# Linear attention in front of a routed MLP: phi(K)^T x summed in fp16 parts and multiplied by Wv once per batch, gate logits as key columns, output bias moved into the expert part

## The chip, the cores and the metric

The kernel runs on one core of one Trainium2 chip. The metric is the device time of the whole program in microseconds (us). The kernel before takes 1902.31 us, the median of three runs (1900.44, 1902.31, 1904.35).

Names used below: PE is TensorE, ACT is ScalarE, DVE is VectorE, POOL is GpSimd, SP is SyncE, which here only issues DMAs.

## The reference, cut to what is computed

```
x: [16 batches, 1024 tokens, 256]            xn = layernorm(x)
Q = phi(xn Wq^T + bq)   K = phi(xn Wk^T + bk)   V = xn Wv^T + bv      phi(t) = elu(t) + 1, 16 heads of 16
KV = sum over tokens of K V^T (per head)      Ksum = sum over tokens of K
attn = (Q KV) / (Q . Ksum + 1e-6), then @ Wo^T + bo
scores = xn @ gate_w (8 experts); softmax over experts; each expert takes its top 256 tokens of a batch
h = gelu(xin @ w1[e]) @ w2[e], weighted by the gate, added back to its tokens; the sum is cast to bfloat16
out = x + attn + moe
```

The precision of fp32 products is reached with fp16 operands split in a high and a low part: three products (high-high, high-low, low-high) stand for one.

## The kernel before, in words

The program has two parts. The first (the attention part) does the layer norm, the attention and the gate, batch by batch; n counts 16 batches (NB), and j the 8 tiles (NT) of 128 tokens in a batch. The second (the expert part) runs 64 quarters: `body(b, ...)` for b from 0 to 15, q from 0 to 3 (five steps in the last). A quarter takes 512 gathered tokens through one expert's two matrices.

All order is written out by hand. Each engine has one in-order list of instructions, and semaphores (`wait_ge(event, at(event, n, k))`) tie the lists together. In the attention part an iteration n works on two batches: the projections of batch n, and the output side of batch m = n - 2 (LAG). The engines' lists for one iteration are:

- PE, `body` at L1385: per tile j `project` (L1262: keys and values in one bank, 6 products of 512 columns and a bias product of 256 columns), `gate` (L1276, four narrow products into bank pG), `sum_kv` of tile j-2 (L1291, fp32, two products of 129 columns, the last one a column of ones that sums phi(K)); `q_part` (L1304) at j = 2, 3, 6, 7; and for batch m `denominators` (j = 0), `turn_kv` (two transposes, j = 1), `fold_o` (j = 2), `reciprocals` (j = 4), and four `output` (after j = 5, 6, 7 and at the end of the iteration).
- ACT, L855: `high` (fp16 high part of x), `keys` (L804: relu of -k from PSUM, a copy of keys and values from PSUM to SBUF, exp), `queries`, `shift`, `sums_out`, `blocks_out`, `folded_out`, and in iterations 1 to 8 (`scan`) four `piece` (maxima of the expert weights).
- DVE, `body` at L1141: `stats_of` and `moments_of` (layer norm of batch n+1), `low`, `k_feature` of tile j-1 (L1035), `q_feature`, `gate_max`, `gate_probs`, `invert`, `split_rest`, `divide`, `add_x`, and from iteration 5 on one part of the top-k search of the first four batches behind every tile (`top_slot`).
- POOL, L754: `centre` (x minus mean, eight per batch), `norm` (L710: variance to 1/sqrt, it waits for `moments_of`), `add_bo` (L748, output bias onto x, four per batch) and `blocks_of` (L730, eight small instructions: value bias, head mask, denominators' operand).

`k_feature` reads keys and exp from SBUF. `project` of tile j needs the copy of tile j-2 out of its PSUM bank (kv_done). SP transposes the fp16 rows by DMA (`turn`), and the transposed buffer of half h comes free when the gates of the batch before are done (`gated`).

In the expert part PE alternates `product1` (6 products of 512 columns) and `product2` (12 of 256 columns). `weigh` on DVE (L1810, four instructions) empties the two PSUM banks of a quarter, and the next quarter's first `product2` waits for it (y_done). From b = 4 on, DVE does `finish(b, q)` (L1830) right ahead of `weigh`: a cast of the expert sum to bfloat16 and one addition onto the attention result. For b < 8 DVE also runs a part of the top-k search behind each `hidden_low` (one of them right ahead of `finish`). These lines set the order there:

```
                        top_slot(b, q, 6)
                        if fin and q < 4:
                            finish(b, q)
...
                        weigh(b, q)
```

## Time and profile before

| | before |
|---|---|
| runs | 1900.44, 1902.31, 1904.35 us |
| median | 1902.31 us |
| profiled execution: span from first to last instruction | 1898.3 us |
| median less span | 4.0 us |
| busy: PE / DVE / ACT / POOL | 98% / 69% / 67% / 54% of the span |
| attention part | to about 542 us of the span |
| expert part | from about 543 us to the end |

The profiled execution is one more execution of the same program, of which the profile gives the span alone, no time of its own; what lies around the span is taken as the 4.0 us between it and the median. "Busy" is the time in which an engine has an instruction in work. A matmul's record includes its latency, so neighbouring records overlap: how long a step of PE or DVE takes is read from one start to the next.

### The profile page before, as it was taken

The numbers are of one execution on the slowest core, as the hardware profiler recorded it, in microseconds if no ns is written. First come the engines' busy times: TensorE is split into PE (matmuls) and PEld (weight loads), VectorE is DVE, ScalarE is ACT, GpSimd is POOL, SyncE is SP. The second block draws the span as 40 slices with busy tenths as digits, with TensorE's granted clock in tenths as the row PEclk, the third lists the DMA queues.
The fourth block names the chain that finished last, engine by engine and source line by source line (L and its number), as shares of the span: only waits on it lengthen the run. The fifth ranks groups of instructions, "written<-read, shape, count | busy, mean of one in ns | idle before, by whom it ended". The sixth has DMA issues, their size and how long they took to land. (4 is left out here: it accounts for less than half of the span.)

```text
span 1898.3 us, 38991 instructions
## 1 busy us (share of the span) xinstructions
PE 1863.2 (98%) x13562; PEld 1269.6 (67%) x13562; DVE 1300.6 (69%) x2611; ACT 1272.2 (67%) x2045; POOL 1026.2 (54%) x947
## 2 busy tenths in 40 slices
PE   6899999999999999999999999999999999999998
PEld 4566666666676666666666666666666666666666
DVE  6678999998857777655787875555555555555556
ACT  6988887777746666666666666666666666666664
POOL 5656565656445555654455455545554554555453
PEclk9999999999999999999999999999999999999999
DMA  6979897989675555666677667576766766676857
GB/s 174 231 221 247 216 251 240 225 236 254 190 191 132 122 120 123 148 179 150 165 157 181 154 158 183 135 177 151 192 152 160 169 143 180 155 187 154 183 120 223
DMA packets 448900, 338.22 MB, mean 178 GB/s; under 512 B 224757, under 2 KB 430330, under 8 KB 448762
## 3 DMA queue, kind: packets, MB, share of 16 engines
q1 hardware_dynamic: 383674, 253.84, 48.5%
q0 software_dynamic: 48864, 66.88, 19.8%
q10 hardware_dynamic: 16224, 15.73, 2.5%
q8 instruction: 77, 1.26, 0.3%
q14 instruction: 61, 0.50, 0.1%
HBM read 185.61 MB, written 100.40 MB: 151 GB/s over the span
## 5 line engine op out<-in xcount | busy, mean ns | idle before, releaser
L1961 PE MATMUL pY<-w2s,hid 128*128 128x256 f16 x6144 | 756.6, 273 | 0.8 <-DVE hid L1806 0.8
L1946 PE MATMUL pH<-xgT,w1s 128*128 128x512 f16 (+1 forms) x3120 | 747.7, 376 | 1.3 <-PEq L324 1.3
L1961 PEld LDWEIGHTS pY<-w2s,hid 128*128 128x128 f16 x6144 | 599.8, 98 | 180.6 <-DVE yo L1822 3.6
L1806 DVE SCALAR_TENSOR_TENSOR hid<-gel,cur,hid 128x512 f16<-128x512 f32 (+1 forms) x520 | 384.6, 740 | 446.4 <-ACT hid L1745 440.8
L1720 POOL DMA_INDIRECT acc<-yo,idx x254 | 405.9, 1598 | 523.0 <-DVE yo L1822 450.0
L1742 ACT ACTIVATE gel<-pH,cur 128x512 f32<-128x512 f32 (+1 forms) x520 | 353.8, 680 | 476.7 <-PE pH L1946 457.2
L1946 PEld LDWEIGHTS pH<-xgT,w1s 128*128 128x128 f16 x3120 | 305.1, 98 | 252.4 <-DMA xgT<-xg 1.6
L1745 ACT ACTIVATE hid<-gel,cur 128x512 f16<-128x512 f32 (+1 forms) x520 | 372.0, 715 | 17.1
L219 POOL DMA_INDIRECT xg<-table,idx x256 | 286.1, 1118 | 112.1 <-issue 58.2
L1270 PE MATMUL pP<-wkv,xT 128*128 128x512 f16 x768 | 201.8, 381 | 7.8 <-DVE bias_rows L981 4.7
L724 POOL TENSOR_SCALAR xm<-xring,moments 128x256 f32<-128x256 f32 x128 | 120.9, 954 | 72.3 <-DVE xhl L1002 72.2
L1822 DVE TENSOR_SCALAR yo<-pY,gains,cur 128x256 f32<-128x256 f32 x256 | 121.6, 538 | 14.0 <-PE pY L1961 12.3
L1270 PEld LDWEIGHTS pP<-wkv,xT 128*128 128x128 f16 x768 | 75.0, 98 | 74.6 <-issue 9.5
L807 ACT ACTIVATE ek<-pP,winv_neg 128x256 f32<-128x256 f32 x128 | 61.2, 478 | 59.4 <-PE pP L1270 58.9
L1317 PE MATMUL pQ<-xT,wq 128*128 128x512 f16 x384 | 93.2, 378 | 2.1 <-ACT qraw L819 2.1
L208 DVE SCALAR_TENSOR_TENSOR w2s<-stage,cur,w2s 128x1024 f16<-128x1024 f32 x64 | 82.8, 1294 | 17.8 <-ACT w2s L200 17.8
L208 DVE SCALAR_TENSOR_TENSOR w1s<-stage,cur,w1s 128x1024 f16<-128x1024 f32 x64 | 82.8, 1294 | 17.9 <-ACT w1s L200 17.9
L752 POOL TENSOR_TENSOR x2ring<-x2ring,rows_all 128x512 f32<-128x512 f32 x64 | 87.1, 1390 | 3.8 <-DMA x2ring<-in_x 3.8
L809 ACT ACTIVATE kv<-pP,winv 128x512 f32<-128x512 f32 x128 | 88.6, 692 | 0.0
L1299 PEld LDWEIGHTS pKV<-kv,phik 128*128 128x128 f32 x512 | 74.4, 191 | 13.9 <-DVE phik L1039 0.7
L1032 DVE TENSOR_TENSOR qring<-qraw,eq 128x512 f32<-128x512 f32 x64 | 50.2, 785 | 46.6 <-ACT eq L821 46.3
L1299 PE MATMUL pKV<-kv,phik 128*128 128x129 f32 x512 | 75.6, 275 | 0.3 <-DVE phik L1039 0.3
(236 smaller groups left out, 1888.5 us busy)
## 6 DMA issues: line engine op xcount, KB each, us to landing
stage<-in_w SPq DMA_DIRECT2D x160, 512.0 KB, 6.4
xring<-in_x SPq DMA_DIRECT2D x16, 1024.0 KB, 6.4
x2ring<-in_x SPq DMA_DIRECT2D x16, 1024.0 KB, 7.6
table<-xhl SPq DMA_DIRECT2D x32, 512.0 KB, 4.1
mix<-x2ring SPq DMA_DIRECT2D x32, 512.0 KB, 3.0
acc<-zeros SPq DMA_DIRECT2D x16, 1024.0 KB, 4.6
fmix<-mix SPq DMA_DIRECT2D x48, 256.0 KB, 3.5
facc<-acc SPq DMA_DIRECT2D x48, 256.0 KB, 4.0
```

Source lines behind the costliest of these rows:

```text
L208: nc.vector.scalar_tensor_tensor(out=part_dst(i, 1, r), in0=staged(r), scalar=cur[i][:, 2 + r // 2:3 + r // 2], in1=part_dst(i, 0, r), op0 ...
L219: nc.gpsimd.indirect_dma_start(xg[i][:, s, :, :, :].rearrange("p a c t -> p (a c t)"), None, table, bass.IndirectOffsetOnAxis(ap=idx[q % 4 ...
L724: g.tensor_scalar(xm[:, j % HALF, :], xring[:, n % XR, j, :], moments[:, j, 0:1], None, ALU.subtract).then_inc(xm_done, 1)
L1270: last = t.matmul(pP[j % 2][:, :], xT[h][:, a, c, cols], wkv[:, b, c, :], start=k == 0 and c == 0, stop=k == 2 and c == DC - 1, skip_group ...
L1299: last = t.matmul(pKV[:, c * (P + 1):(c + 1) * (P + 1)], phik[:, j % 4, c * P:(c + 1) * P], kv1[:, j % 4, DC + c, :], start=j == 0 and c = ...
L1720: g.indirect_dma_start(acc, bass.IndirectOffsetOnAxis(ap=idx[q][:, s:s + 1], axis=0), yo[i][:, s, :], None, compute_op=ALU.add).then_inc(a ...
L1742: a.activation(gel[:, hc % 2, w], pH[hc % 4][:, w], ACT.Gelu_apprx_tanh, scale=c[:, 0:1]).then_inc(gel_done, 1)
L1745: a.activation(hid[:, hc % 4, 0, w], gel[:, hc % 2, w], ACT.Copy, scale=c[:, 1:2]).then_inc(hhi_done, 1)
L1806: v.scalar_tensor_tensor(out=hid[:, hc % 4, 1, w], in0=gel[:, hc % 2, w], scalar=cur[expert_of(b, q)][:, 1:2], in1=hid[:, hc % 4, 0, w], o ...
L1822: last = v.tensor_scalar(yo[i][:, s, :], pY[s // 2][:, s % 2, :], gains[:, ds(column_of(b * 4 + quarter_of(b, q)) * 4 + s, 1)], cur[expert ...
L1946: last = t.matmul(pH[hc % 4][:, tok], w[:, aw, c, hc * P:(hc + 1) * P], xgT[i][:, ad, c, tok], start=k == 0 and c == 0, stop=k == 2 and c ...
L1961: last = t.matmul(pY[s // 2][:, s % 2, :], hid[:, hc % 4, ad, s * P:(s + 1) * P], w[:, aw, hc, :], start=hc == 0 and k == 0 and s % 2 == 0 ...
```

## The change

- `project` computes keys and gate logits only. The bank holds 272 columns (GATED): 256 keys, 8 logits of the high weights and 8 of the low. Seven products: 2 of 272 columns, 1 of 256 (bias), 2 of 256, 2 of 264. `gate` is gone.
- phi is written as max(k + 1, exp(min(k, 0))). The 1 is added into the key bias, ACT makes relu(1 - k') and exp, and `k_feature` on DVE is one scaled maximum that reads the bank in PSUM. The bank is free only after it: `project` of tile j waits for k_done of tile j-2. ACT no longer copies keys and values.
- phi(K) is split in two fp16 parts: the high one on ACT (`key_high`, behind `keys` of the next tile), the low one on POOL (`key_low`). `sum_kv` multiplies them by the fp16 rows of x (`xhl`): 6 products of 256 columns and 4 of one column (the sums). It waits for klo_done. The rows' buffers come free only after `sum_kv` (`high` waits for kv_used).
- Once per batch `fold_v` (4 fp32 products of 128 columns) multiplies by Wv, in place of the two transposes. The head mask and the value bias are put in by DVE: `blocks_out` (256 columns from PSUM, times the mask) and `folded_out` (2 instructions of 256 columns), both of which were plain copies on ACT. POOL's `blocks_of` shrinks to `sums_of` (2 small instructions).
- `add_bo` is gone from POOL. The output bias is added in the expert part: an instruction of 512 columns in every `finish` (DVE), and 8 of 1024 columns on POOL during b = 4 for the rows finished last.
- `sum_kv` of the last two tiles of a batch moves to tiles 0 and 1 of the next iteration. POOL's list is interleaved tile by tile, with `norm(n+1)` at j = 3, ahead of `key_low(n, 2)`. `later_consts` moves ahead of the first `norm`.

```diff
@@ sync
-                        value = held(sp, at(gated, n - 1, h))
+                        value = held(sp, at(q_proj, n - 1, 2 * h + 1))
@@ gpsimd
+                def key_low(n, j):
+                    pool.wait_ge(khi_done, at(khi_done, n, j))
+                    g.tensor_tensor(phk[:, j % 4, 1, :], phik[:, j % 4, 0:D], phk[:, j % 4, 0, :], ALU.subtract).then_inc(klo_done, 1)
...
                 for n in range(NB):
-                    for j in range(HALF, NT):
-                        centre(n, j)
-                    if n >= LAG:
-                        for u in range(4):
-                            add_bo(n - LAG, u)
-                    if n < NB - 1:
-                        norm(n + 1)
-                        for j in range(HALF):
-                            centre(n + 1, j)
...
+                    for j in range(NT):
+                        if j < HALF - 1:
+                            centre(n, HALF + 1 + j)
+                        if nxt and j == HALF - 1:
+                            norm(n + 1)
+                        if nxt and j >= HALF - 1:
+                            centre(n + 1, j - (HALF - 1))
+                        if j > 0:
+                            key_low(n, j - 1)
+                        elif n > 0:
+                            key_low(n - 1, NT - 1)
+                        if n > 0 and j == HALF:
+                            sums_of(n - 1)
@@ scalar
                 def keys(n, j):
                     act.wait_ge(proj, at(proj, n, j))
                     act.wait_ge(k_done, at(k_done, n, j - 2))
-                    a.activation(ek[:, j % 2, :], pP[j % 2][:, 0:D], ACT.Relu, scale=winv_neg[:, 2:3]).then_inc(kneg_done, 1)
+                    a.activation(ek[:, j % 2, 0:D], pP[j % 2][:, 0:D], ACT.Relu, scale=winv_neg[:, 2:3], bias=1.0).then_inc(kneg_done, 1)
+                    act.wait_ge(kneg_done, at(kneg_done, n, j))
+                    a.activation(ek[:, j % 2, 0:D], ek[:, j % 2, 0:D], ACT.Exp, scale=-1.0, bias=kln[:, 0:1]).then_inc(ek_done, 1)
+
+                def key_high(n, j):
+                    act.wait_ge(k_done, at(k_done, n, j))
                     act.wait_ge(kv_used, at(kv_used, n, j - 4))
-                    a.activation(kv1[:, j % 4, :, 0:P], pP[j % 2][:, :].rearrange("p (c t) -> p c t", c=2 * DC),
-                                 ACT.Copy, scale=winv[:, 2:3]).then_inc(kv_done, 1)
-                    act.wait_ge(kneg_done, at(kneg_done, n, j))
-                    a.activation(ek[:, j % 2, :], ek[:, j % 2, :], ACT.Exp, scale=-1.0).then_inc(ek_done, 1)
+                    a.activation(phk[:, j % 4, 0, :], phik[:, j % 4, 0:D], ACT.Copy).then_inc(khi_done, 1)
@@ vector
                 def k_feature(n, j):
-                    dve.wait_ge(kv_done, at(kv_done, n, j))
-                    dve.wait_ge(kv_used, at(kv_used, n, j - 4))
+                    dve.wait_ge(klo_done, at(klo_done, n, j - 4))
                     dve.wait_ge(ek_done, at(ek_done, n, j))
...
+                    v.scalar_tensor_tensor(out=phik[:, j % 4, :], in0=pP[j % 2][:, 0:GATED], scalar=KUNIT, in1=ek[:, j % 2, :],
+                                           op0=ALU.mult, op1=ALU.max).then_inc(k_done, 1)
+
+                def blocks_out(m, alone=False):
+                    dve.wait_ge(kv_turned, at(kv_turned, m))
+                    v.tensor_tensor(kvT[:, :, :], bank_kv(m, alone)[:, 0:DC * P].rearrange("p (c t) -> p c t", c=DC),
+                                    head_mask[:, :].unsqueeze(1).to_broadcast([P, DC, P]), ALU.mult).then_inc(kvT_done, 1)
+
+                def folded_out(m, alone=False):
+                    dve.wait_ge(mo_mm, at(mo_mm, m))
+                    for c in range(DC):
+                        last = v.scalar_tensor_tensor(out=mo_of(m)[:, c, :], in0=bvo[:, c, :], scalar=ksring[:, m % 2, c:c + 1],
+                                                      in1=banks_mo[not alone][:, c * D:(c + 1) * D], op0=ALU.mult, op1=ALU.add)
+                    last.then_inc(mo_done, 1)
...
                             if j == 2:
                                 split_rest(m)
+                                blocks_out(m)
+                            if j == 3:
+                                folded_out(m)
@@ tensor
+                    bank = pP[j % 2]
+                    for c in range(DC):
+                        t.matmul(bank[:, 0:GATED], xT[h][:, 0, c, cols], wkg[:, c, :], start=c == 0, stop=False, skip_group_check=True)
+                    t.matmul(bank[:, 0:D], bias_lhs[:, :], bias_rows[:, :], start=False, stop=False, skip_group_check=True)
+                    for c in range(DC):
+                        t.matmul(bank[:, 0:D], xT[h][:, 0, c, cols], wk_low[:, c, :], start=False, stop=False, skip_group_check=True)
+                    for c in range(DC):
+                        last = t.matmul(bank[:, 0:D + E], xT[h][:, 1, c, cols], wkg[:, c, 0:D + E], start=False, stop=c == DC - 1,
+                                        skip_group_check=True)
                     last.then_inc(proj, 1)
...
+                def sum_kv(n, j):
                     h, jj = divmod(j, HALF)
...
+                    pe.wait_ge(klo_done, at(klo_done, n, j))
                     if j == 0:
                         pe.wait_ge(kv_out, at(kv_out, n, -1))
...
                     for c in range(DC):
...
+                        for b in range(2):
+                            t.matmul(pS[:, c:c + 1], phk[:, j % 4, b, c * P:(c + 1) * P], one_col[:, 0:1],
+                                     start=j == 0 and c == 0 and b == 0, stop=j == NT - 1 and b == 1, skip_group_check=True)
+                    for k, (a, b) in enumerate(((0, 0), (0, 1), (1, 0))):
+                        for c in range(DC):
+                            last = t.matmul(pKV[:, c * D:(c + 1) * D], xhl[h][:, jj, a, c, :], phk[:, j % 4, b, :],
+                                            start=j == 0 and k == 0 and c == 0, stop=j == NT - 1 and k == 2, skip_group_check=True)
                     last.then_inc(kv_used, 1)
@@ expert part, vector
                     v.tensor_copy(fffn[:, i, :, :], facc[:, i, :, :]).then_inc(fin_cast, 1)
+                    v.tensor_tensor(fmix[:, i, :, :], fmix[:, i, :, :], bo_all[:, :].unsqueeze(1).to_broadcast([P, 2, D]), ALU.add).then_inc(fin_bo, 1)
                     dve.wait_ge(fin_cast, at(fin_cast, 4 * b, q - FIN0))
+                    dve.wait_ge(fin_bo, at(fin_bo, 4 * b, q - FIN0))
                     v.tensor_tensor(fmix[:, i, :, :], fmix[:, i, :, :], fffn[:, i, :, :], ALU.add).then_inc(fin_done, 1)
@@ expert part, gpsimd, behind the wait for y_done of its quarter
+                        if isinstance(b, int) and b == G1:
+                            if q == 0:
+                                pool.wait_ge(lmix_in, at(lmix_in, 0, LP - 1))
+                            for k in (2 * q, 2 * q + 1):
+                                g.tensor_tensor(lmix[:, piece_of(k), :], lmix[:, piece_of(k), :],
+                                                bo_all[:, :].unsqueeze(1).to_broadcast([P, HALF, D]), ALU.add).then_inc(lbo_done, 1)
```

## Rows read from the trace of the kernel before

**Rows 1.** Windows, iterations 7 to 9: length; busy PE, PEld, DVE, ACT, POOL; clock; DMA.

```profile
250.00:300.00 50.00, 49.94 (x403) 34.26 (x402) 45.31 (x119) 42.87 (x92) 29.83 (x32) 1.00 0.83 233
```

**Rows 2.** Timeline of PE, one iteration: start us, us, engine, line, operation, count.

```profile
211.75 0.23 PE L1350 MATMUL pE<-zpart,spread 64*128 64x128 bf16 x1
...
220.41 0.24 PE L1286 MATMUL pG<-wg,xT 128*128 128x16 f16 x4
220.51 1.45 PE L1317 MATMUL pQ<-xT,wq 128*128 128x512 f16 x6
221.80 0.61 PE L1299 MATMUL pKV<-kv,phik 128*128 128x129 f32 x4
222.25 0.38 PE L1270 MATMUL pP<-wkv,xT 128*128 128x512 f16 x1
...
223.65 1.89 PE L1365 MATMUL pO<-mo,qz 128*128 128x256 f32 x8
...
229.84 0.38 PE L1270 MATMUL pP<-wkv,xT 128*128 128x512 f16 x1
...
242.94 0.61 PE L1299 MATMUL pKV<-kv,phik 128*128 128x129 f32 x4
```

**Rows 3.** Instructions by line and shape, attention part: total busy us, mean ns, idle before.

```profile
L809 ACT ACTIVATE kv<-pP,winv 128x512 f32<-128x512 f32 x128 | 88.6, 692 | 0.0
...
L1039 DVE SCALAR_TENSOR_TENSOR phik<-kv,ek 128x256 f32<-128x256 f32 x128 | 59.2, 462 | 18.7 <-ACT ek L812 16.7 <-PE pKV L1299 1.8
...
L249 DVE MAX8 topv<-rows 64x8 f32<-64x512 f32 x32 | 21.7, 677 | 0.0
...
L1062 DVE TENSOR_TENSOR qz<-qring,pQ 128x512 f32<-128x512 f32 x15 | 10.1, 674 | 0.0
```

**Rows 4.** Timeline of DVE, the same stretch and the next iteration.

```profile
230.14 0.68 DVE L1068 TENSOR_TENSOR x2ring<-x2ring,pD 128x512 f32<-128x512 f32 x1
...
239.59 0.62 DVE L929 BATCH_NORM_AGGREGATE moments<-stats 128x2 f32<-128x6 f32 x8
...
258.89 1.31 DVE L1014 TENSOR_TENSOR gsub<-logits,gmax 128x32 f32<-128x32 f32 x1
```

**Rows 5.** Timeline of POOL, two iterations; idle before it and its releaser in brackets.

```profile
208.65 0.91 POOL L714 TENSOR_SCALAR veps<-moments 128x8 f32<-128x8 f32 x1 [7.81 <-DVE moments L929]
...
240.38 0.91 POOL L714 TENSOR_SCALAR veps<-moments 128x8 f32<-128x8 f32 x1 [7.79 <-DVE moments L929]
...
243.03 3.86 POOL L724 TENSOR_SCALAR xm<-xring,moments 128x256 f32<-128x256 f32 x4
...
248.04 1.00 POOL L740 TENSOR_TENSOR kvm<-kvm,kvring 128x128 f32<-128x128 f32 x2
...
258.88 5.42 POOL L752 TENSOR_TENSOR x2ring<-x2ring,rows_all 128x512 f32<-128x512 f32 x4
```

**Rows 6.** Timeline of DVE, then PE, end of an expert quarter with top-k parts.

```profile
922.80 0.69 DVE L1835 TENSOR_TENSOR fmix<-fmix,fffn 128x512 f32<-128x512 f32 x1
923.41 1.89 DVE L1822 TENSOR_SCALAR yo<-pY,gains,cur 128x256 f32<-128x256 f32 x4
...
924.62 1.57 PE L1961 MATMUL pY<-w2s,hid 128*128 128x256 f16 x12
```

**Rows 7.** Timeline of DVE, then PE, end of an expert quarter without them.

```profile
1215.87 0.42 DVE L1833 CAST fffn<-facc 128x512 bf16<-128x512 f32 x1
1216.33 0.69 DVE L1835 TENSOR_TENSOR fmix<-fmix,fffn 128x512 f32<-128x512 f32 x1
1217.07 1.90 DVE L1822 TENSOR_SCALAR yo<-pY,gains,cur 128x256 f32<-128x256 f32 x4
...
1218.74 1.47 PE L1961 MATMUL pY<-w2s,hid 128*128 128x256 f16 x12
```

**Rows 8.** Timeline of PE, its first projections after an idle stretch.

```profile
20.01 0.58 PE L1270 MATMUL pP<-wkv,xT 128*128 128x512 f16 x1 [4.70 <-DVE bias_rows L981]
...
20.60 2.69 PE L1270 MATMUL pP<-wkv,xT 128*128 128x512 f16 x6
```

More of the change, by code:

```diff
@@ L17 @@
+import math
 from contextlib import ExitStack
@@ L771, in _ @@
+                key_low(NB - 1, NT - 1)
+                sums_of(NB - 1)
                 pool.wait_ge(picks_done, at(picks_done, 0))
@@ L880, in _ @@
                             queries(n, j - 2)
-                        if j == 2 and s2:
-                            folded_out(m)
                         if j == 5:
@@ L1222, in _ @@
                 m = NB - LAG
+                blocks_out(m, True)
                 weight_low(dve, 0, 3, 0)
+                folded_out(m, True)
                 for c in range(DC):
@@ L1232, in _ @@
                 split_rest(m + 1)
+                blocks_out(m + 1, True)
                 add_x(m, 1, True)
+                folded_out(m + 1, True)
                 gate_probs(NB - 1, 1)
@@ L1366, in output, with fold_v @@
                     last.then_inc(out_mm, 1)
-                def turn_kv(m, alone=False):
+                def fold_v(m, alone=False):
+                    pe.wait_ge(kv_out, at(kv_out, m))
                     if not alone:
@@ L1371, in turn_kv @@
                     for c in range(DC):
-                        last = t.transpose(bank_kv(m, alone)[:, c * P:(c + 1) * P], kvm[:, c, :], ident[:, :])
+                        for cc in range(DC):
+                            last = t.matmul(bank_kv(m, alone)[:, c * P:(c + 1) * P], wvT[:, cc, c * P:(c + 1) * P],
+                                            gring[:, m % 2, cc, c * P:(c + 1) * P], start=cc == 0, stop=cc == DC - 1)
                     last.then_inc(kv_turned, 1)
@@ L1392, in body @@
                             if j == 1:
[L1393 to L1396 removed]
+                                fold_v(m)
+                        if n == 1 and j == 0:
+                            bias_blocks()
                         if j in (2, 3):
[L1398 removed]
                             q_part(n, j - 2)
```

247 lines of the change are left out of this document (114 added, 133 removed).

## The prediction

> **What bounds the kernel now.** I read the page first (busy shares, the 40 slices), then the windows by stage, then the timeline of each engine over one iteration and over one quarter of the expert part. PE is busy 98% of the span, so the first reading is that only PE's work counts. The windows show that this is true but narrow: in a stretch of iterations 7 to 9 PE is busy 49.94 of 50 us, and DVE 45.31 and ACT 42.87 beside it [rows 1]. DVE is thus at 28.8 us of each iteration of 31.73 us (the same POOL instruction starts at 208.65 and at 240.38 [rows 5]). Take 10% off PE and DVE is the next bound. The reader is to see one more thing in the POOL timeline: `norm` sits waiting for DVE's moments for 7.8 us in every iteration [rows 5]. Today nothing that PE needs soon is behind it.
>
> **PE's work.** A projection takes 1.40 us (222.25 to 223.65) for 3328 columns, a `sum_kv` 0.45 us (221.80 to 222.25), four gate products 0.10 us (220.41 to 220.51) [rows 2]. By the same rate the new projection of 1840 columns takes 0.77 (-0.63), and the new `sum_kv` 1536 columns at 0.65 plus four one-column products at 0.10, that is 0.75 (+0.30). `fold_v`, four fp32 products of 128 columns, is twice what two of 129 take, 0.90; the transposes that it replaces are at most 0.45 now, so it adds 0.45 to 0.90, and I take 0.65. Per iteration: 31.73 - 8 x 0.63 - 8 x 0.10 + 8 x 0.30 + 0.65 = 28.9 us. If PE stayed the bound in all 16, that would be 45 us less, and 1857 us. That is what the change is worth on PE alone.
>
> **What takes its place in iterations 5 to 14.** `sum_kv(n, 2)` now needs `key_low(n, 2)`, and in POOL's list that stands behind `norm(n+1)` and one `centre`. `norm` needs DVE's `moments_of`. DVE gets there along its own list, which starts the iteration with an `add_x` that waits for the last `output` on PE. So there is a loop through three engines. I walk it from PE's first projection (229.84 [rows 2]):
> - DVE's `add_x` starts 0.30 later (230.14), and the moments 9.45 after that (239.59) [rows 4]. DVE has no idle time in this stretch.
> - Three DVE instructions of 256 columns are new ahead of the moments, `blocks_out` and two of `folded_out`. The nearest row is the `k_feature` of today, 256 columns at 0.46 us [rows 3], of which some 0.06 overlaps its neighbour: 3 x 0.40 = 1.2. A 512-column instruction from PSUM takes 0.67 [rows 3], so the upper bound is 2.0. `k_feature` itself changes its source and gains 16 columns: nothing to 0.2 each, I take nothing.
> - From the start of the moments to the first `centre` behind `norm`: 239.59 to 243.03, 3.44 us [rows 4, 5]. One `centre`: a quarter of 3.86, 0.97 [rows 5].
> - `key_low`, POOL, 256 columns, two inputs. Rows on either side: 128 columns at 0.50, 512 at 1.36 (1.00 for two, 5.42 for four) [rows 5]. I take 0.75.
>
> Sum: 0.30 + 9.45 + 1.2 + 3.44 + 0.97 + 0.75 = 16.1 us. PE is there at 12.3: today's third `sum_kv` starts 13.10 after the projection (242.94 [rows 2]), less five projections' 3.15 and four gates' 0.40, plus 0.60 for `sum_kv` 0 and 1, 1.50 for the two moved in from the iteration before, and 0.65. So PE stands still for 3.8 us. `reciprocals` is queued behind it, DVE's `divide` waits for that, and the output products follow. What PE then has left: from `reciprocals` to the next first projection takes 18.09 today (211.75 to 229.84 [rows 2]); less three projections' 1.89 and four gates' 0.40, and three `sum_kv` at 0.75 for five at 0.45, it is 15.8. The loop is 16.1 + 0.75 + 15.8 = 32.7 us, against 31.73: +1.0 in each of ten iterations, **+10 us**. The 2.8 us saved per iteration is gone in the wait, and it doesn't come back, since DVE's next walk starts from PE's end.
>
> The ends of this term: shorter by 1.0 if `key_low` costs 0.5 and DVE is a little quicker; longer by up to 2.3 with the upper prices. POOL works in a stretch in which it idled, and DVE then waits for it: with POOL's long additions beside it a 32-column DVE instruction took 1.31 us (258.89 [rows 4]), twice a 512-column one. The Trainium skill states this too (GPSIMD Engine Reference, Key points): POOL shares its SBUF interfaces with VectorE, and instructions with two SBUF inputs contend. By that rule `k_feature`, with one input now in PSUM, gets a little lighter and the others in the stretch a little heavier; the sum above charges neither.
>
> **The other iterations.** In iterations 2 to 4 DVE runs no part of the search, of which four pieces (0.68 each [rows 3]) lie ahead of the moments: 16.1 - 2.7 = 13.4, and the loop 30.0: -1.7 each, -5 us. Iterations 0 and 1 have no output side and are bound by ACT's chain; ACT loses a copy of 0.69 per tile [rows 3] and gets one of half the columns: -1 each, -2 us. Iteration 15 has no `norm` ahead of it (PE's 2.8 us come through), but the changeover gets `blocks_out`, `folded_out`, the key parts and `fold_v` in line, about 2 us: together -1. ACT is no bound anywhere: it was at 27.2 us per iteration [rows 1] and loses more than it gets. The start is even: later_consts falls in time in which POOL waits. Attention part: -2 - 5 + 10 - 1 = **+2 us**.
>
> **The expert part.** It looks free, DVE being little over half busy. But the new instruction stands in the one place that matters, between DVE's last `hidden_low` and `weigh`, and PE's next `product2` needs `weigh`. Its cost is one 512-column addition, 0.69 [rows 6]: today cast to addition is 0.46 (1215.87 to 1216.33 [rows 7]), then it is 0.35 plus 0.73: +0.62.
> - Quarters with search parts: `weigh` starts at 923.41 and ends at 925.30, 0.68 after PE's `product2` began at 924.62, and those twelve products take 1.57 instead of 1.47 [rows 6, 7]. PE already waits 0.10. All of the 0.62 is added. There are 10 such quarters with a `finish`: +6.2.
> - Quarters without: addition to `weigh` takes 0.74 instead of 0.61 [rows 6, 7], so `weigh` waits 0.13 for PE and starts only 0.49 later. It ends 0.23 after the `product2` began (1218.97 against 1218.74 [rows 7]); by the rows with the wait, 0.58 is when PE begins to feel it. Slack 0.35, so 0.14 per quarter, 38 of them: +5.3.
>
> Together **+11.5 us**, between 0 and 30 (48 x 0.62 without any slack). POOL's eight bias additions in b = 4, some 2.7 us each by twice the 512-column row [rows 5], put 5.4 us in each of four quarters of some 21 us (64 of them between 543 and 1898), of which POOL, 54% busy, has over 9 free; the next gather is due a quarter later. Nothing. If that cover were gone, at most 4 x 5.4 us.
>
> **Sum.** 1902.3 + 2 + 11.5 = 1915.8. Against the profile's own span: 1898.3 + 13.5 = 1911.8, and the 4.0 us between that span and the median stay.
>
> **Rivals.**
> - *DVE's load is all that counts* (faster; chance 0.25). If the key part of tile 2 is ready before PE wants it, or DVE gets to the moments sooner since it no longer idles for the queries of the iteration before, then DVE's load sets the pace: 28.8 + 1.2 = 30.0, with a little for `k_feature` 30.1. Ten iterations give -16, the others -8, the expert part +11.5: 1890. For it: DVE idles 3 us of each iteration today, and in this chain every term can be too long. Against it: the order of POOL's list. It decides where `sum_kv(n, 2)` can start before 14.5 us into its iteration instead of 16.1: -8 + 10 x (start - 15.1) + 11.5 is then below -3.8.
> - *The bias addition is hidden* (same; 0.12). If the slack in the expert quarters is larger than 0.35, or the addition runs while `weigh` waits anyway, the +11.5 falls away and the rest stays: 1904. The waits of 0.10 in the quarters with search parts speak against it.
> - *PE's clock falls in the new waits* (slower; 0.13). After PE had stood still 4.70 us, its first projections ran at half rate: six products of 512 columns in 2.69 us [rows 8], where `q_part` takes 1.29 for six (220.51 to 221.80 [rows 2]). That is the level of 1.2 GHz instead of 2.4, and it cost 1.4 us. A wait of 3.8 us is near that. If each of the ten brings it: +14, 1930. The Trainium skill (TensorE: Matmul & The Clock Gate, HAM oscillation) states the rule: idle stretches of PE bring the slow clock back, every time.
> - *The narrower products don't run shorter* (slower; 0.03), each hung on its weight load. Then `project` saves nothing and the loop grows by 3 x 0.63 or more: 1935 and above. The twelve products of 256 columns in 1.47 us [rows 7] speak against it.
>
> The rest, 0.47, is the forecast. **Range**: its own is 1905 to 1928. For 8 in 10 it must reach into the first rival: 1891 to 1930. Runs of this kernel differ by 4 us, so 0.2% (3.8 us) is about what a measurement can tell from no change. Faster: the first rival, 0.25, and 0.01 from the second. Same: most of the second and the low end of the forecast, 0.13. Slower: 0.61.
>
> **What would show it.** Right: projections of 0.77 us; PE idle some 3 to 4 us ahead of the third `sum_kv`, released by POOL's key part, in iterations 5 to 14, and about 1 us in 2 to 4; batches 32 to 33 us apart; quarters 0.14 us longer, those with search parts 0.62, but only from b = 4 on. Wrong: batches 30 us apart with DVE near 100% busy; granted clock under 1.00 after iteration 2; expert quarters unchanged. The weakest term is DVE's way to the moments: 1 us on it is 10 us in the total.

## The result

The changed kernel takes 1942.68 us (median of four runs, 1939.81 to 1943.81), the kernel before 1902.11 (four runs of it beside these): a ratio of 1.0215, with a 95% interval of 1.02 to 1.0229. It is slower by 40.6 us. The forecast was 1916 us with a range of 1891 to 1930; the sign was right, the size was not.

The profiled execution of the changed kernel has a span of 1938.1 us against 1898.3. The page, busy times of the engines:

```profile
PE 1851.5 (96%) x13916; PEld 1284.5 (66%) x13916; DVE 1331.5 (69%) x2713; ACT 1262.5 (65%) x2030; POOL 1011.6 (52%) x925
```

Where do the 39.8 us of span lie? The first product of the expert part starts at 560.60 us, where it was at 543.43: the attention part lost 17.2 us, the expert part 22.6. Within the attention part I read the start of `denominators` in each iteration, before and after. An iteration is counted from its `denominators` to the next ones. Iterations 0 and 1 together are 1.9 longer; 2 to 4 are 2.3 shorter; 5 to 14 are 15.4 longer; 15 and the changeover are 2.2 longer.

The windows of one iteration each (the end of iteration 0 with iteration 1, then iterations 7, 13 and 4; columns: stretch, its length, busy time of PE, weight loads, DVE, ACT, POOL, then PE's granted clock, DMA share, GB/s):

```profile
43.00:73.98 30.98, 23.22 (x164) 15.65 (x165) 17.19 (x64) 23.72 (x53) 15.83 (x20) 0.83 0.61 170
233.66:268.04 34.38, 30.84 (x285) 23.85 (x284) 28.19 (x81) 26.88 (x58) 16.53 (x20) 0.95 0.82 214
436.17:469.00 32.83, 29.28 (x286) 22.55 (x285) 28.10 (x81) 22.83 (x49) 16.54 (x20) 1.00 0.84 231
137.01:167.48 30.47, 29.71 (x289) 22.99 (x288) 23.66 (x67) 26.55 (x58) 16.12 (x20) 1.00 0.92 243
```

Iteration 13 takes 32.8 us, where 32.7 were forecast. Iteration 7 does the same work and takes 34.4: its mean granted clock is 0.95, since PE ran from 250.01 to 253.40, right behind its second wait, at 1.2 GHz in place of 2.4 (granted clock 0.50 there, 1.00 before and behind it). Iterations 6 to 9 are of that kind, and half of 11 (33.5 us). The timeline of PE inside iteration 7:

```profile
238.66 1.46 PE L1346 MATMUL pQ<-xT,wq 128*128 128x512 f16 x6
241.82 1.13 PE L1410 MATMUL pD<-woT,kvT 128*128 128x256 f32 x4 [1.71 <-DVE kvT L1058]
242.79 0.24 PE L1325 MATMUL pS<-one_col,phk 128*128 128x1 f16 x4
...
243.55 0.40 PE L1307 MATMUL pP<-wkg,xT 128*128 128x272 f16 x2
...
244.33 1.46 PE L1346 MATMUL pQ<-xT,wq 128*128 128x512 f16 x6
...
249.17 0.25 PE L1325 MATMUL pS<-one_col,phk 128*128 128x1 f16 x4 [1.84 <-POOL phk L741]
```

PE stands still twice: 1.71 us ahead of `fold_o`, which waits for DVE's `blocks_out`, and 1.84 us ahead of `sum_kv(n, 2)`, which waits for POOL's key part. The second was forecast (with 3.8 us), the first was not. In iterations 12 and 13, at full clock, the two waits are 1.71 and 1.84 us too. POOL and DVE at the same time:

```profile
244.75 0.91 POOL L722 TENSOR_SCALAR veps<-moments 128x8 f32<-128x8 f32 x1 [2.79 <-DVE moments L930]
245.75 1.67 POOL L725 TENSOR_TENSOR rpow<-veps,minus_half 128x8 f32<-128x8 f32 x1
247.40 0.94 POOL L732 TENSOR_SCALAR xm<-xring,moments 128x256 f32<-128x256 f32 x1
248.30 0.81 POOL L741 TENSOR_TENSOR phk<-phik,phk 128x256 f16<-128x256 f32 x1
```

```profile
240.24 0.41 DVE L1053 SCALAR_TENSOR_TENSOR phik<-pP,ek 128x272 f32<-128x272 f32 x1
240.57 0.27 DVE L1076 TENSOR_TENSOR zrest<-zz,zpart 128x128 f32<-128x128 f32 x1
...
241.35 0.42 DVE L1058 TENSOR_TENSOR kvT<-pD,head_mask 128x256 f32<-128x256 f32 x1
...
243.96 0.62 DVE L930 BATCH_NORM_AGGREGATE moments<-stats 128x2 f32<-128x6 f32 x8
```

This answers to [rows 4, 5]: `norm` waits 2.8 us for the moments, where it waited 7.8, and now the key part of tile 2 is behind it. `blocks_out` has had its product since 237.1, but stands at 241.35 in a list without a gap.

In the expert part, the starts of `weigh` show three kinds of quarter. Plain ones are those without a part of the search. The first row and the last are 25 of them apart (528.19 us):

```profile
1268.82 1.90 DVE L1858 TENSOR_SCALAR yo<-pY,gains,cur 128x256 f32<-128x256 f32 x4
...
1797.01 1.90 DVE L1858 TENSOR_SCALAR yo<-pY,gains,cur 128x256 f32<-128x256 f32 x4
```

That is 21.13 us each, against 20.84 before: +0.29, twice the forecast 0.14. Quarters with search parts take 21.61 against 20.94: +0.67, forecast 0.62. And b = 4 has a quarter of 25.08 and one of 22.81, which were not forecast: together 4.7 over their neighbours. POOL, DVE and PE in the longer one:

```profile
987.88 5.04 POOL L1753 TENSOR_TENSOR lmix<-lmix,bo_all 128x1024 f32<-128x1024 f32 x2 [1.91 <-DVE yo L1858]
```

```profile
989.63 1.00 DVE L210 COPY cur<-scales 128x5 f32<-128x5 f32 x1
990.55 2.92 DVE L1842 SCALAR_TENSOR_TENSOR hid<-gel,cur,hid 128x512 f16<-128x512 f32 x1
...
1009.17 0.43 DVE L1869 CAST fffn<-facc 128x512 bf16<-128x512 f32 x1 [2.18 <-DMA facc<-acc]
```

```profile
993.53 1.49 PE L1999 MATMUL pY<-w2s,hid 128*128 128x256 f16 x12 [1.01 <-DVE hid L1842]
...
1011.96 1.30 PE L1999 MATMUL pY<-w2s,hid 128*128 128x256 f16 x8 [2.63 <-DVE yo L1858]
```

A `hidden_low` that takes 0.74 us elsewhere took 2.92 beside POOL's additions, and PE waited 1.01 us for it. The accumulating transfers are issued only behind POOL's additions of 5.04 us. At the end of the quarter the cast of `finish` waits 2.18 us for the loaded sums, and PE waits a second time, 2.63 us for `weigh`. That the late issue is what made the load late is read from the order of these rows.

### The profile page after: what moved, and what is told of

The parts are those of the page before. It is cut to its first block and busy times, and to the rows that moved or that the text cites. A ratio compares the mean times of both kernels' runs of the same rounds, so it can differ in the third digit from the quotient of the medians.

```text
span 1938.1 us, 39960 instructions
## 1 busy us (share of the span) xinstructions
PE 1851.5 (96%) x13916; PEld 1284.5 (66%) x13916; DVE 1331.5 (69%) x2713; ACT 1262.5 (65%) x2030; POOL 1011.6 (52%) x925
## 5 line engine op out<-in xcount | busy, mean ns | idle before, releaser
L1842 DVE SCALAR_TENSOR_TENSOR hid<-gel,cur,hid 128x512 f16<-128x512 f32 (+1 forms) x520 | 394.4, 759 | 431.2 <-ACT hid L1781 316.6
L1756 POOL DMA_INDIRECT acc<-yo,idx x254 | 424.3, 1671 | 498.7 <-DVE yo L1858 422.3
L225 POOL DMA_INDIRECT xg<-table,idx x256 | 279.2, 1091 | 111.8 <-issue 59.3
L741 POOL TENSOR_TENSOR phk<-phik,phk 128x256 f16<-128x256 f32 x128 | 93.4, 730 | 220.8 <-ACT phk L819 220.7
L1329 PE MATMUL pKV<-phk,xhl 128*128 128x256 f16 x768 | 106.7, 276 | 0.0
L1017 DVE SCALAR_TENSOR_TENSOR xhl<-xm,rstd,xhl 128x256 f16<-128x256 f32 x128 | 70.4, 552 | 7.3 <-ACT xhl L806 7.3
L206 ACT ACTIVATE w2s<-stage,cur 128x1024 f16<-128x1024 f32 x64 | 72.5, 1133 | 0.0
L206 ACT ACTIVATE w1s<-stage,cur 128x1024 f16<-128x1024 f32 x64 | 72.5, 1132 | 0.0
L1329 PEld LDWEIGHTS pKV<-phk,xhl 128*128 128x128 f16 x768 | 65.8, 97 | 6.9
```

The costliest lines, as they stand in the source:

```text
L206: nc.scalar.activation(part_dst(i, 0, r), staged(r), ACT.Copy, scale=cur[i][:, 2 + r // 2:3 + r // 2]).then_inc(whi_done, 1)
L225: nc.gpsimd.indirect_dma_start(xg[i][:, s, :, :, :].rearrange("p a c t -> p (a c t)"), None, table, bass.IndirectOffsetOnAxis(ap=idx[q % 4 ...
L1329: last = t.matmul(pKV[:, c * D:(c + 1) * D], xhl[h][:, jj, a, c, :], phk[:, j % 4, b, :], start=j == 0 and k == 0 and c == 0, stop=j == NT ...
L1756: g.indirect_dma_start(acc, bass.IndirectOffsetOnAxis(ap=idx[q][:, s:s + 1], axis=0), yo[i][:, s, :], None, compute_op=ALU.add).then_inc(a ...
L1842: v.scalar_tensor_tensor(out=hid[:, hc % 4, 1, w], in0=gel[:, hc % 2, w], scalar=cur[expert_of(b, q)][:, 1:2], in1=hid[:, hc % 4, 0, w], o ...
```

## The experiments

All times are medians; the kernel before ran beside them at 1900.4 to 1902.0 us. "The changed kernel" is at 1942.7.

**1. The key part of tile 2 ahead of most of `norm`.**

```diff
                     g.tensor_scalar(veps[:, :], moments[:, :, 1], 1e-5, None, ALU.add).then_inc(veps_done, 1)
+                    if between is not None:
+                        key_low(*between)
...
-                            norm(n + 1)
+                            norm(n + 1, between=(n, j - 1))
```

> The changed kernel with one step moved in GpSimd's list: the key part of tile 2 now stands between the first instruction of norm and its pow, not behind the whole norm and one centre. Theory (the order of GpSimd's list makes the second wait of PE): sum_kv(n, 2) no longer waits 1.84 us, so iterations 5 to 14 lose 1.8 us each, and in iterations 6 to 9 and 11, where the granted clock was 0.95, another 1.5 us each: 18 + 8 = 26 us less, 1917 us; clock 1.00 in all iterations from 2 on. The wait of fold_o (1.71 us) stays. Rival 1 (the loop through the moments sets the period, whatever stands in GpSimd's list; norm's pow is now 0.8 us later, and with it the next batch's tiles): the wait shows up elsewhere, 1938 to 1950 us. Rival 2 (only the clock matters): 8 us less, 1935.

Measured: 1922.03 us (ratio to before 1.0117, 1.0098 to 1.0136), 20.6 less than the changed kernel. Iterations 6 to 14 are 31.5 to 32.0 us each, where they were 32.8 to 34.5. The window of iteration 7, and PE's waits from 170 to 500 us (us in total, times, longest), here and then in the changed kernel:

```profile
230.74:262.28 31.54, 29.27 (x285) 22.55 (x284) 27.79 (x81) 26.77 (x58) 16.57 (x20) 1.00 0.87 233
```

```profile
PE pD L1413 <- DVE kvT L1061: 16.1, 10, 1.8
PE pS L1328 <- POOL phk L743: 5.6, 10, 0.6
```

```profile
PE pS L1325 <- POOL phk L741: 16.3, 9, 1.8
PE pD L1410 <- DVE kvT L1058: 16.1, 10, 1.8
```

The wait for POOL shrank from 1.8 to 0.56, the one for `blocks_out` stayed, the granted clock is 1.00 again in iterations 2 to 14 of the profiled execution. (One of the four runs took 1927.2 us at a mean clock of 0.991, the others 0.995.) Both rivals fall: the place in POOL's list was a cause of its own (1.3 us per iteration against those at full clock, where 1.8 were expected), and the clock came on top (1.6 more in those that had lost it).

**2 and 3. `blocks_out` one tile earlier, alone and with move 1.**

```diff
                             if j == 2:
                                 split_rest(m)
-                                blocks_out(m)
...
+                        if s2 and j == 1:
+                            blocks_out(m)
                         if j == 1 and n > 0:
                             gate_probs(n - 1, 1)
```

> The changed kernel with one step moved in DVE's list: blocks_out stands one tile earlier, behind the first low part of tile 5 and ahead of the k_feature and split_rest that it stood behind. Theory (the two waits of PE are two readings of one chain: DVE and GpSimd reach the key part of tile 2 at their own pace, so what PE gains at fold_o it gives back at sum_kv(n, 2)): the wait of 1.71 us at fold_o goes, the one of 1.84 at sum_kv(n, 2) grows to 3 to 3.5; time 1939 to 1948 us, the longer single wait costing clock in more iterations. Rival (the two waits are independent and add up): 1.7 us less in ten iterations, 1925 us.

> Both moves together (the key part of tile 2 inside norm, blocks_out one tile earlier). Theory (list orders alone hold PE back): both waits go, 3.5 us in each of ten iterations and 8 us of clock, 43 us less: 1900 us, batches 29.3 us apart, which is about PE's own work. Rival (DVE's load is the next bound: 28.2 us busy per iteration plus what it idles between its steps): the waits reappear behind DVE, batches 30.5 to 31.5 us apart, 1912 to 1922 us.

Measured: alone 1952.0 us (1.0267, 1.0246 to 1.0289), 9.3 more than the changed kernel; with move 1 1921.17 (1.0105, 1.0088 to 1.0122), no more than move 1 gives alone. PE's waits from 170 to 500 us, first with `blocks_out` alone, then with both:

```profile
PE pS L1326 <- POOL phk L741: 40.9, 20, 3.2
```

```profile
PE pS L1329 <- POOL phk L743: 20.3, 20, 1.4
```

The wait of `fold_o` is gone in both, and the time is not. In the first there is a wait of 1.0 to 1.4 at `sum_kv(n, 0)`, and the one at `sum_kv(n, 2)` grew from 1.8 to 2.9 (3.2 at most); it cost clock (iterations 6 to 14 take 33.4 to 36.2 us). In the second `sum_kv(n, 0)` waits 1.3 and `sum_kv(n, 3)` 0.8, since each key part follows ACT's copy, and that follows a `k_feature` in DVE's list. So the two waits were two readings of one chain: without the one at `fold_o` an iteration takes 31.35 us, with it 31.54. The rival that had DVE behind it came true, in its length (30.5 to 31.5) and in its time. In the timeline of DVE with both moves, DVE is idle three times per iteration, always for the queries' exp on ACT:

```profile
401.46 0.69 DVE L1050 TENSOR_TENSOR qring<-qraw,eq 128x512 f32<-128x512 f32 x1 [0.75 <-ACT eq L831]
...
413.24 0.69 DVE L1050 TENSOR_TENSOR qring<-qraw,eq 128x512 f32<-128x512 f32 x1 [1.47 <-ACT eq L831]
...
417.80 0.69 DVE L1050 TENSOR_TENSOR qring<-qraw,eq 128x512 f32<-128x512 f32 x1 [0.58 <-ACT eq L831]
```

**4. Those idle stretches filled with DVE work that is ready.**

```diff
-                        if j in (3, 4):
-                            q_feature(n, j - 3)
+                        if j == 3:
+                            q_feature(n, 0)
                         if j == HALF:
                             gate_max(n, 0)
+                            q_feature(n, 1)
...
                                 stats_of(n + 2, 1)
-                            q_feature(n, 2)
+                                stats_of(n + 2, 2)
+                                stats_of(n + 2, 3)
...
+                    q_feature(n, 2)
                     k_feature(n, NT - 1)
...
                     gate_max(n, 1)
-                    if n + 2 < NB:
-                        stats_of(n + 2, 2)
-                        stats_of(n + 2, 3)
+                    top_slot(n, NT)
                     q_feature(n, 3)
...
-                    top_slot(n, NT)
```

> Both moves of list order (the key part of tile 2 inside norm, blocks_out one tile earlier), and DVE's q_feature steps put behind other ready work: q_feature(n, 1) behind gate_max(n, 0), q_feature(n, 2) behind a search piece and two more statistics, q_feature(n, 3) behind a search piece. Theory (with both moves made, DVE stands idle 2.8 us of each 31.35 at three q_feature, and that idle time, not its work of 28.5 us, is what PE's last waits of 2.2 us come from): DVE's waits shrink to under 1 us, batches come 29.2 to 29.6 us apart, ten iterations give 18 to 21 us: 1901 us. Rival (the period is set by the chain through the queries, PE to ScalarE to DVE to PE, so the place in the list does not matter): batches stay at 31.3, 1921 us.

Measured: 1911.04 us (1.0048, 1.0031 to 1.0065), 10.1 less than with the two moves, half of what was expected. Most iterations are 30.4 us apart. The window of one:

```profile
400.00:430.40 30.40, 29.19 (x286) 22.48 (x285) 28.79 (x82) 22.52 (x49) 16.38 (x21) 1.00 0.99 248
```

DVE is at 28.8 of 30.4 and PE at 29.2. Filling DVE's idle time was worth 1 us per iteration and not the 2 that were expected: from 170 to 500 us it still waits 9.7 us for the queries' exp, where it waited 29.0. Iterations 3 and 4, which run no search, are at 30.0, against 31.44 and 31.88 before; the shortest that any version showed are 29.87 (`blocks_out` moved alone).

**5. Without the output bias in the expert part.** Both `finish`'s addition on DVE and POOL's eight are left out (the bias is then missing from the output).

> The changed kernel without the output bias in the expert part (left out altogether: neither DVE's addition in finish nor GpSimd's eight additions in b = 4). Theory (all that the expert part lost hangs on these instructions): that part goes back from 1377.5 to 1355 us, the total to 1920. Rival 1 (the expert part is longer because it now starts at another phase of its queues): it stays above 1370, total 1935. Rival 2 (DVE's slack was as I had it and the rest is contention by other work): 11.5 less, 1931.

Measured: 1920.6 us (1.0105, 1.0089 to 1.0122), 22.1 less. Plain quarters are at 20.84 again, those with search parts at 20.94, and no quarter of b = 4 is longer than before. The expert part takes 1354.6 us, where the kernel before has 1354.9. The whole loss of the expert part hangs on these instructions.

**6 and 7. `finish` one `hidden_low` earlier; in the first of the two, POOL's additions moved ahead of its wait as well.**

```diff
+                        if fin and q < 4:
+                            finish(b, q)
                         if not ends(q, last):
                             hidden_low(b, q + 1, 0)
                         top_slot(b, q, 6)
-                        if fin and q < 4:
-                            finish(b, q)
```

> The changed kernel with its attention part untouched; in the expert part finish (cast, bias addition, addition) stands ahead of the last but one hidden_low of the quarter, where DVE is idle 1.85 us, not right ahead of weigh; and GpSimd's eight additions in b = 4 stand ahead of its wait for y_done, in which it idles 7 us, not behind it. Theory (the bias addition costs only where it delays weigh, GpSimd's only where they delay the accumulating transfers): quarters come 20.84 us apart again, with search parts 20.94 or a little less, no long quarters in b = 4: expert part 1355 us, total 1920. Rival 1 (fmix and facc have not landed 2.6 us earlier, and DVE waits for them ahead of a hidden_low): quarters 21.3 and more, total 1945 or more. Rival 2 (GpSimd's additions cost by slowing DVE, wherever they stand): 2 to 5 us remain in b = 4, total 1923 to 1925.

> The changed kernel with finish one hidden_low earlier, and GpSimd's eight additions where the change has them (behind its wait for y_done). Theory (the 18 us that the run with both moves lost in b = 3 to 5 came from GpSimd's additions: while one runs, DVE stands still, and in their new place they fell beside a 1024-column weight step and a hidden_low that PE waits for; finish itself is free in its new place): plain quarters 20.84, those of b = 4 about 21 with one of 24 to 25: 1942.7 - 22.6 + 5 = 1925 us. Rival (the early finish waits for its transfers in the quarters with search parts): quarters of 23 and more in b = 4 and 5 with the additions back in place, total 1938 to 1945.

Measured: with both moves 1939.94 us (1.0203, 1.0186 to 1.022), 20 more than expected; with `finish` alone 1927.01 (1.0127, 1.011 to 1.0144), 2 more than expected. In both, the plain quarters are 20.84 us: the addition is free where DVE is idle, and `weigh` waits 0.7 to 1.1 us for PE. But with POOL's additions in their new place the five quarters around b = 4 take 25.2, 24.1, 25.4, 27.3 and 23.4 us. DVE and POOL in the first of these:

```profile
914.78 6.37 DVE L214 SCALAR_TENSOR_TENSOR w1s<-stage,cur,w1s 128x1024 f16<-128x1024 f32 x1 [0.29 <-issue]
```

```profile
915.40 4.67 POOL L1745 TENSOR_TENSOR lmix<-lmix,bo_all 128x1024 f32<-128x1024 f32 x2
```

A weight step of 1.28 us took 6.37: 5.09 longer, a little more than the 4.67 of POOL's two additions together. It ended 1.08 us behind them. The Trainium skill (SBUF — State Buffer, Who interferes with whom) says that a DVE instruction with two SBUF inputs and a GpSimd one that reads SBUF exclude each other for the whole instruction; this trace agrees, with the 6.37 us. Which of the two goes first is not seen from these rows: DVE's starts 0.62 earlier and still stands through both of POOL's. The second run, which differs from the first in POOL's additions alone, is 13 us faster, so their place cost that much. With the additions in the change's place one quarter of 25.97 remains.

**8. The output bias back in the attention part.** Four additions of 512 columns per batch on POOL, at tiles 5 to 7 of the iteration ahead of their use, in its idle stretches; none in the expert part.

> The changed kernel with one part undone: the output bias is added as before the change, in the attention part by GpSimd (four additions of 512 columns per batch, put in its idle stretches at tiles 5 to 7 of the iteration before they are needed), and nothing in the expert part. Theory: the expert part gives back its 22 us, and the attention part pays little, since GpSimd is idle there: 0 to 0.3 us per iteration by contention with DVE: total 1920 to 1925. Rival (two-input additions on GpSimd slow DVE beside them, and DVE's way to the moments is the loop that sets the period): each addition of 1.36 us costs DVE 0.4, 1.6 us per iteration, 16 us in ten: 1936.

Measured: 1923.08 us (1.0113, 1.0096 to 1.013), 19.6 less than the changed kernel. The expert part is that of the run without bias (1354.9 us), and the attention part pays nothing that shows for 64 additions: in the two profiled executions it takes 562.2 us with them and without, and the 2.5 us between the medians are less than either kernel's four runs spread. DVE is busy 28.81 us of an iteration of 32.83 with the additions, and 28.10 of the same 32.83 in the changed kernel. It had idle time to lose.

**9. PE's `bias_blocks` later.** New in the change are two products that fold Wo onto the value bias, once, at tile 0 of iteration 1. PE waits there, and what follows is slow (six products of 256 columns take 1.44 us here and 0.81 in iteration 7):

```profile
45.98 2.07 PE L1297 MATMUL pD<-woT,kvT 128*128 128x256 f32 x4 [4.38 <-DVE kvT L1003]
...
48.00 1.44 PE L1329 MATMUL pKV<-phk,xhl 128*128 128x256 f16 x6
```

```diff
-                        if n == 1 and j == 0:
+                        if n == 1 and j == 3:
                             bias_blocks()
...
-                        if j == 1 and n == 1:
+                        if j == 4 and n == 1:
                             bias_blocks_out()
```

> The changed kernel with PE's bias_blocks of iteration 1 (the two products that fold Wo onto the v bias, new in the change) at tile 3 instead of tile 0, and ScalarE's copy of them at tile 4. Theory (PE waits 4.4 us there for DVE's blocks, and then runs at the slow clock for 6 us; this is why iterations 0 and 1 got 1.9 us longer and not 2 shorter): the wait is gone, denominators of iteration 2 start 4 to 6 us earlier, 1937.5 us. Rival (iterations 0 and 1 are bound by ScalarE's chain anyway): ScalarE's queue absorbs it, 0 to 2 us less, 1942.

Measured: 1938.32 us (1.0197, 1.0178 to 1.0217), 4.4 less, though the runs spread from 1936 to 1944. The medians alone don't show it. In the profiled executions the `denominators` of iteration 3 start at 104.2 us here and at 103.3 in the last version of experiment 10, which has this move too; in the ten executions of the changed kernel and its versions that don't have it, they start at 106.1 to 109.3. The direction is shown, its size only as 2 to 5 us. Waits of 1.3 to 1.4 us at `sum_kv` take the place of part of the 4.38.

**10. All list orders, nothing left out.** The three moves of the attention part, `finish` early, `bias_blocks` late, and POOL's eight additions given to DVE in the last body:

> All moves together: the two list orders, the q_feature steps, finish one hidden_low earlier, GpSimd's additions ahead of the wait for y_done. Nothing is left out. If the parts are independent and each theory holds: 1942.7 - 43 - 22 = 1878 us, faster than the kernel before by 1.2%. Rival (what one stage gains comes back in another, as with blocks_out alone): 1900 or more.

This first version had POOL's additions ahead of its wait and `bias_blocks` in its old place: 1906.17 us (1.0025, 1.0014 to 1.0035), where 1878 was expected; what it lacks is the 18 us that experiment 6 lost around b = 4, and the 10 that experiment 4 fell short of. The version without that fault:

```diff
+                            if last and q in (1, 2) and hc < 6:
+                                k = 4 * (q - 1) + hc - 2
+                                if k == 0:
+                                    dve.wait_ge(lmix_in, at(lmix_in, 0, LP - 1))
+                                v.tensor_tensor(lmix[:, piece_of(k), :], lmix[:, piece_of(k), :],
+                                                bo_all[:, :].unsqueeze(1).to_broadcast([P, HALF, D]), ALU.add).then_inc(lbo_done, 1)
```

> Nothing left out. All list orders of the attention part (key part of tile 2 inside norm, blocks_out one tile earlier, q_feature behind ready work, bias_blocks late), finish one hidden_low earlier, and the bias of the last 4096 rows added by DVE in the last body in its idle time, not by GpSimd. Theory (every loss of the change is a place in a list, but DVE's load stays): attention part 31.6 us less as with the three orders, another 4 for bias_blocks, expert part 22.6 less: 1884.5 us, 0.9% faster than the kernel before. Rival 1 (the additions by DVE in the last body come in the way of PE): +1 to 5. Rival 2 (the start's gain is not additive): 1888.

Measured: 1884.84 us (1883.12 to 1885.28), ratio to before 0.9907 (0.989 to 0.9923). It is the only version here that is faster than the kernel before beyond its interval, by 17 us, and 58 us faster than the changed kernel. Of the profiled executions, its attention part is 16.4 us shorter than that of the kernel before (527.0 against 543.4), its expert part 1.7 longer.

**11. The kernel before with only `finish` moved,** to see how much of that is not the change's:

> The kernel before, with only the move of finish one hidden_low earlier in the expert part. It shows how much of what the last version gained is this move and not the change. Theory (in the kernel before finish delayed weigh but almost never PE: 0.10 us in the quarters with search parts, and 0.5 to 1 at the end): 2 us less, 1900 us, within what can be measured. Rival (the move is worth as much here as in the changed kernel, since weigh comes earlier): 5 us less or more, 1897 or below.

Measured: 1899.04 us against 1900.37 (0.9993, 0.9984 to 1.0002): no difference that can be measured. So the 17 us are not the move of `finish`. Of the list orders of the attention part only those were moved in the changed kernel; no run moves them in the kernel before. There PE is busy 49.94 of 50 us [rows 1], which leaves an order little to win in iterations 7 to 9, so the changed arithmetic, with lists that fit it, is the likely source. This is argued and not shown.

## Why the prediction was too low

The loop of the attention part was right. What failed are these steps of the sum. PE's clock stood in it at nothing, as a rival of 0.13, and cost 7.2 us. POOL's additions in b = 4 stood at nothing and cost 4.7. The slack of a plain expert quarter was taken as 0.35 us and gave 0.14 per quarter, where 0.29 were measured: 5.1 more. And the iterations outside of 5 to 14 were to gain 8 us together and lost 1.8. The cause of the last is shown for a part alone.

**PE's steps: right.** A projection takes 0.78 us (243.55 to 244.33), forecast 0.77; `sum_kv` 0.76 (242.79 to 243.55), forecast 0.75; `fold_v` 0.89 (236.23 to 237.12), its upper end, forecast 0.65. PE is busy 29.3 us in iteration 13, forecast 28.9. Iterations 3 and 4 of the later versions come near it: 30.0 us, with 0.6 to 0.7 of waits still in them.

**The loop through `norm`: right in kind and place.** `sum_kv(n, 2)` starts 16.4 us behind the first projection (249.17 against 232.79; forecast 16.1), and the iterations at full clock take 32.8 us (forecast 32.7). This is not a sum in which errors cancel: `add_x` starts at 0.39 (0.30), the moments 10.78 behind it (10.65), the first `centre` 3.44 behind them (3.44), and `centre` and `key_low` take 0.90 and 0.87 (0.97 and 0.75). The wait of 3.8 us was there, but in two parts, 1.71 and 1.84: I had walked PE's list from step to step by its work alone, and did not ask when DVE's new `blocks_out`, which PE needs two tiles earlier, comes up in DVE's list. For the time this changed little (0.2 us per iteration), as experiment 3 shows, since both waits end in the same chain.

**PE's clock: the forecast had it as a rival of 0.13, and it holds almost half of what iterations 5 to 14 lost.** I took it that a wait must be near 4.7 us. Two waits of 1.71 and 1.84 us, with 5.5 us of work between them, were enough in iterations 6 to 9 and in part of 11. They were not in 12 and 13, which have the same two waits, nor in 14 (1.71 and 1.57). So the "every time" that the prediction repeats does not hold for waits of this length. An iteration that loses clock takes 1.6 us more, where the rival had 1.4. Of the 15.4 us that iterations 5 to 14 lost, 7.2 are the clock (four at 1.6, and 0.8 in iteration 11) and 8.2 the loop, for which 10 were forecast. This split is that of one execution. The profiled executions of experiments 5, 6 and 7 have the same attention part. In those of experiments 5 and 6 it is iterations 6, 8, 12, 13, 14 and part of 9 that are slow, and the expert part starts at 562.2 us, against 560.6. In that of experiment 7 it is 5 to 8, 10, 12, 13, 14 and part of 11, and the expert part starts at 569.7. It is 9.1 us later, of which 2.4 are there at iteration 2 already, so some 7 us more can hang on the clock from one execution to the next. What decides it within one kernel stays open.

**Iterations 0 and 1: the step "ACT loses a copy, -2 us" left out `bias_blocks`.** I called the start even, after looking at POOL's queue alone. PE's new step waits 4.4 us for DVE's masks. Experiment 9 gives 2 to 5 us of it back. The measured +1.9 itself is no more than executions differ by: the `denominators` of iteration 2 start at 72.6 to 76.3 us in four executions with this start, and at 72.1 and 74.1 in two of the start before. Iterations 2 to 4 gained 2.3 in place of 5: iteration 2 nothing, 3 and 4 1.0 and 1.4, with waits of 1.08 and 0.65 at `sum_kv(n, 2)`. The changeover with iteration 15 cost 2.2 in place of -1; I did not take it apart, and its cause stays open.

**The expert part: the term was mis-sized twice.** (a) The slack of a plain quarter. `weigh` moved by 0.7 us against PE and not by 0.49: DVE's cast itself starts 0.18 later against PE's products than in [rows 7] (1267.09 against 1267.17, before 1215.87 against 1216.13), and the chain from cast to `weigh` grew by 0.53. By the prediction's own measure, PE feels all beyond 0.58: the 0.23 of [rows 7] and 0.7 make 0.93, and less 0.58 that is 0.35, measured 0.29 (0.20 in the execution of experiment 9, whose expert part is the same). In 36 quarters this makes 10.4 us in place of 5.3. (b) "POOL's additions in b = 4: nothing" was wrong: 4.7 us. I checked POOL's time and not DVE's. The row for it was there: a 32-column instruction of 1.31 us beside POOL's additions [rows 4]. I read it as a slow-down of a small instruction. It fits DVE standing still: the same instruction takes 0.19 us in the changed kernel, where POOL no longer adds beside it, and one of POOL's four additions takes 1.36. Next to an addition of 2.5 us that means up to 2.5 us in `hidden_low`, for which PE waits.

Summed for the two profiled executions, what came on top of the forecast of +13.5: clock 7.2, the loop -1.8, iterations 0 and 1 3.9, iterations 2 to 4 2.7, iteration 15 and the changeover 3.2, plain quarters 5.1, quarters with search parts 0.5, b = 4 4.7, and the last full quarter 0.8 (12.56 us against 11.76). With the 13.5 that is 39.8, the difference of the spans. The "DVE's load" rival (0.25) is not refuted as a mechanism. With the list orders mended an iteration takes 30.4 us (the rival said 30.1), and what PE still waits for are key parts that hang on DVE's list. But its number is in part luck: it counted 30.0 us of DVE work, and DVE is busy 28.1 in iteration 13 of the changed kernel and 28.8 after experiment 4, as it no longer stands beside `add_bo` (with those additions back, experiment 8, it is 28.8 in place of 28.1). With PE at 29.2 of the 30.4, no run shows that DVE's load alone binds. In its last sentence the rival also has a slip: at a start of 14.5 us its sum gives -2.5 and not below -3.8.

## What to carry to other kernels

When work is taken from the bounding engine, write down for each new step on the other engines which instruction of the old bound waits for it and where it stands in its own in-order list; a step that is moved earlier alone can make things worse (1942.7 to 1952.0 us here), since the wait only turns up at the next step of its chain. Put small additions where the engine's timeline shows a wait for another engine, not just ahead of the instruction that the bound waits for: the same 512-column addition cost 0.29 to 0.67 us there and nothing one step earlier. And before giving long two-input work to GpSimd, ask what DVE has to deliver in that time.

## What the runs showed of the hardware that I had not expected

- A DVE instruction with two SBUF inputs stood still while POOL added two SBUF operands: 1.28 us became 6.37 beside 4.67 us of additions, and 0.74 became 2.92 where 2.37 us of the 5.04 were left when it started.
- The mean granted clock fell to 0.95 in iterations in which PE never stood still for more than 1.84 us at once, but not in all that have the same two waits. It was 1.00 in iterations 2 to 14 of the profiled execution in which the longer of the two was 1.71 and the other 0.56.
